# Turning the token tiles of two feed-forward stages without the matrix engine

## The reference

```python
x = x + 0.5 * ffn(layernorm(x), weight, bias, lora_A, lora_B, starts)
x = x + attention(layernorm(x), wq_a, q_a_ln_w, wq_b, wkv_a, kv_a_ln_w, wkv_b, wo)
x = x + 0.5 * ffn(layernorm(x), weight, bias, lora_A, lora_B, starts)

def ffn(x, ...):            # x is (2, 1024, 1024)
    y = x @ weight.T + bias
    lo = (x @ A.T) @ Bw.T   # rank 16, the adapter is chosen per batch
    return y + lo if the batch uses an adapter else y
```

## Time and profile before

| | |
|---|---|
| median of 3 runs | 1862.01 us (1861.92 to 1864.57) |
| the profiled execution: its time, its span | 1863.24 us, 1861.4 us |
| PE busy | 1783.3 us, 96% of the span |
| DVE, ACT, POOL busy | 66%, 54%, 44% |
| mean granted clock of PE | 0.987 |
| first stage, tile 2's matmuls to tile 15's | 69.75 to 241.97 us |
| second stage, the same | 1692.87 to 1857.62 us |
| DMA | 216.29 MB, 35.7% of 16 engines' span |

### The profile page before, as it was taken

One profiled execution on the slowest core, in us unless ns is written; L12 is line 12 of the kernel. 1 busy time (PEld: TensorE's weight loads), 2 busy tenths in 40 slices (PEclk: granted clock), 3 DMA queues, 4 the chain that ended last, 5 costly groups with the idle time before them and its releaser, 6 DMA issues. The chain is left out here.

```text
span 1861.4 us, 43728 instructions
## 1 busy us (share of the span) xinstructions
PE 1783.3 (96%) x15472; PEld 1416.4 (76%) x15472; DVE 1221.7 (66%) x2454; ACT 1007.1 (54%) x2137; POOL 813.6 (44%) x585
## 2 busy tenths in 40 slices
PE   5999969999999999999999999998899999989999
PEld 4788869877777777777777777775688888867887
DVE  5655448688887888878888787888533344435552
ACT  2221037788888888888888888887200001112110
POOL 3231211376766767667676676764200000024211
PEclk9999979999999999999999999999999999999999
DMA  6542162322222222212222122226855555525321
GB/s 215 199 163 102 60 178 92 75 82 59 65 87 66 74 57 64 87 61 79 57 64 87 56 83 57 64 81 210 306 181 196 202 206 207 193 91 168 126 90 57
DMA packets 141152, 216.29 MB, mean 116 GB/s; under 512 B 28192, under 2 KB 97952, under 8 KB 139040
## 3 DMA queue, kind: packets, MB, share of 16 engines
q1 hardware_dynamic: 141088, 215.43, 35.7%
HBM read 139.10 MB, written 76.28 MB: 116 GB/s over the span
## 5 line engine op out<-in xcount | busy, mean ns | idle before, releaser
L1318 PE MATMUL psS<-keyT,q 128*128 128x512 f32 (+2 forms) x2304 | 462.5, 349 | 12.4 <-issue 3.5
L1318 PEld LDWEIGHTS psS<-keyT,q 128*128 128x128 f32 x2304 | 377.6, 190 | 95.0 <-issue 33.1
L1436 DVE CUSTOM_DVE_ANT_0 prob<-psS,mask 128x640 f32<-128x640 f32 (+7 forms) x512 | 380.2, 750 | 80.2 <-PE psS L1318 55.3
L1385 ACT ACTIVATE prob<-prob,negmax 128x640 f32<-128x640 f32 (+7 forms) x512 | 393.2, 769 | 66.8 <-DVE negmax L1436 62.5
L1446 DVE STREAM_TRANSPOSE pT<-prob 128x640 f32<-128x640 f32 (+7 forms) x512 | 375.1, 761 | 81.9 <-PE psV L1335 77.4
L1111 PE MATMUL psS<-o_w,o_o 128*128 128x512 f32 x1536 | 350.8, 390 | 7.5 <-DVE o_w L1079 4.6
L1111 PEld LDWEIGHTS psS<-o_w,o_o 128*128 128x128 f32 x1536 | 288.8, 188 | 69.2 <-issue 7.4
L469 PE MATMUL f_psy<-f_weff,f_xT 128*128 128x512 f32 x1344 | 315.6, 393 | 0.0
L469 PEld LDWEIGHTS f_psy<-f_weff,f_xT 128*128 128x128 f32 x1344 | 250.8, 188 | 55.8
L1335 PE MATMUL psV<-pT,val 32*64 32x512 f32 (+3 forms) x8192 | 264.9, 407 | 4.7 <-DVE pT L1446 4.7
L633 POOL TENSOR_TENSOR pT<-pT,cosT 64x512 f32<-64x512 f32 x124 | 160.1, 1291 | 244.8 <-ACT pT L628 235.4
(11 more groups left out here) (118 smaller groups left out, 1710.7 us busy)
## 6 DMA issues: line engine op xcount, KB each, us to landing
o_parts<-pT SPq DMA_DIRECT2D x128, 256.0 KB, 3.0
wo<-in_wo SPq DMA_DIRECT2D x16, 1024.0 KB, 5.0
o_in<-o_parts SPq DMA_DIRECT2D x32, 512.0 KB, 6.7
o_o<-o_parts SPq DMA_DIRECT2D x32, 512.0 KB, 7.3
o_o<-row_scales SPq DMA_DIRECT2D x32, 512.0 KB, 8.2
f_xt<-in_x SPq DMA_DIRECT2D x16, 512.0 KB, 4.3
f_w_in<-in_w SPq DMA_DIRECT2D x16, 512.0 KB, 6.2
w_sum<-f_w_in SPq DMA_DIRECT2D x16, 512.0 KB, 5.3
```

Of the source, the lines that this page charges most:

```text
L1318: ins = nc.tensor.matmul(psS[:, slot, start + x0:start + x1], q[:, e, a, t * P:(t + 1) * P], k.keyT[:, m, b * S + x0:b * S + x1], start=(i ...
L1385: nc.scalar.activation(row, row, ACT.Exp, bias=negmax[:, n % 8:n % 8 + 1], scale=-1.0, accum_out=rowsum[:, column(n, s):column(n, s) + 1]) ...
L1436: nc.vector.tensor_tensor_reduce(out=prob[:, n % RING, 0:width], in0=place(n), in1=k.mask[:, S - width:S], scale=-1.0, scalar=LARGEST, op0 ...
```

## The change

Tiles 0 and 1 are still turned on PE. For tiles 2 to 15 of each stage the turning is made from three others:

- x is loaded with its rows in another order (`load_x` with `c a d`): partition 4c + a holds token 32a + c.
- DVE normalises into `normal[j]`. Four SBUF-to-SBUF transfers of 128 KB each (`move`) copy 256 columns of all 128 partitions into one strip of 32 partitions. DVE then turns each 32x32 block (`flip`). After it partition 32q + r holds feature 256q + 32t + r of the tokens.
- ACT takes the high part from `normal[j]` in SBUF, POOL the low part. DVE had it before.

The weights are laid out on the host in the same order of features, and tiles 0 and 1 are normalised into it. `xo` is no longer made from `f.xt`: x is loaded a second time into `xo[j]` (`load_sum`), and POOL adds the bias in place. So `f.xt` is free earlier, and x is loaded four tiles ahead. In the first stage there is one buffer `normal` and one for the strips; in the second there are two buffers `normal` and a new tensor for the strips. Some semaphores of set-up code are merged. The core of the diff:

```diff
@@ class Front / ffn_phase @@
-        nc.vector.tensor_scalar(self.xn[:, j, :], self.xt[:, j, :], self.mv[:, j, 0:1], self.rstd[:, j, :],
+        nc.vector.tensor_scalar(self.xn[:, j, :].rearrange("p (t q r) -> p q t r", q=GROUPS, t=DT),
+                                self.xt[:, j, :].rearrange("p (q t r) -> p q t r", q=GROUPS, t=DT), self.mv[:, j, 0:1], self.rstd[:, j, :],
                                 ALU.subtract, ALU.mult).then_inc(self.normed, 1)
...
+        if early is None:
+            normal, strips, ahead = (f.xn[:, 0, :], f.xn[:, 0, :]), f.xn[:, 1, :], 1
+        else:
+            normal, strips, ahead = (f.xn[:, 0, :], f.xn[:, 1, :]), c.sb(tag + "strips", [P, D])[:], 2
...
+        def turned_over(j, g):
+            return normal[j].rearrange("p (a t c) -> p t a c", a=GROUPS, t=DT)[:, 4 * g:4 * g + 4]
+        def split(j, part, g):
+            return f.xT[:, j, part, 4 * g:4 * g + 4, :].rearrange("p t (a c) -> p t a c", a=GROUPS)
@@ sync @@
             def load_x(m, jm):
-                sp.dma_start(f.xt[:, jm, :], src_d[bass.ds(m * P, P), :]).then_inc(f.x_in[jm], 16)
+                rows = src_d[bass.ds(m * P, P), :]
+                if later(m, 2):
+                    rows = rows.rearrange("(a c) d -> c a d", a=GROUPS)
+                sp.dma_start(f.xt[:, jm, :], rows).then_inc(f.x_in[jm], 16)
+            def load_sum(m, jm):
+                sp.dma_start(xo[:, jm, :], src_d[bass.ds(m * P, P), :]).then_inc(xo_in[jm], 16)
+            def move(m, jm):
+                sp.wait_ge(f.normed, m + 1)
+                if later(m, 3):
+                    sp.wait_ge(flipped, m - 2)
+                for q in range(GROUPS):
+                    sp.dma_start(strips[32 * q:32 * q + 32, :],
+                                 normal[jm][:, WIDTH * q:WIDTH * q + WIDTH]).then_inc(moved, 16)
...
+                if i == 6:
+                    move(2, 0)
+                    load_x(4, 0)
             def step(n, j, b, pieces, has):
...
-                if has(3):
-                    sp.wait_ge(f.normed, n + 2)
-                    sp.wait_ge(with_bias, n + 2)
-                    load_x(n + 3, (j + 1) % 2)
+                if has(2):
+                    move(n + 2, j)
+                if has(4):
+                    load_x(n + 4, j)
+                if has(1):
+                    sp.wait_ge(stored[(j + 1) % 2], loads_of(n - 1, (j + 1) % 2 if later(n, 2) else 0))
+                    load_sum(n + 1, (j + 1) % 2)
                 for i in pieces:
                     renew(i)
@@ gpsimd @@
             def add_bias(n, j):
+                if later(n, 2):
+                    pool.wait_ge(xo_in[j], (n - j) * 8)
+                    nc.gpsimd.tensor_tensor(xo[:, j, :], xo[:, j, :], bias_half[:], ALU.add).then_inc(with_bias, 1)
+                    return
...
             def step(n, j, b, pieces, has):
+                jm = (j + 1) % 2
+                if has(1):
+                    for g in range(2):
+                        pool.wait_ge(f.hi, n * 2 + g + 3)
+                        nc.gpsimd.tensor_tensor(split(jm, LO, g), turned_over(jm, g), split(jm, HI, g).bitcast(F32),
+                                                ALU.subtract).then_inc(f.lo, 1)
                 pieces_low(pieces)
                 if has(1):
-                    add_bias(n + 1, (j + 1) % 2)
+                    add_bias(n + 1, jm)
@@ scalar @@
                 if has(1):
-                    f.split_hi(nc, act, n + 1, (j + 1) % 2, product, 2)
+                    jm = (j + 1) % 2
+                    act.wait_ge(product, n * 2)
+                    act.wait_ge(flipped, n)
+                    for g in range(2):
+                        nc.scalar.activation(split(jm, HI, g), turned_over(jm, g), ACT.Copy).then_inc(f.hi, 1)
@@ tensor @@
             def step(n, j, b, pieces, has):
-                if has(1):
-                    f.turn(nc, pe, k.ident, n + 1, (j + 1) % 2)
@@ vector @@
+            def normalised(n, j):
+                f.invert(nc, dve, n, j)
+                dve.wait_ge(f.lo, (n - ahead) * 2 + 2)
+                dve.wait_ge(f.inv, n + 1)
+                nc.vector.tensor_scalar(normal[j], f.xt[:, j, :], f.mv[:, j, 0:1], f.rstd[:, j, :],
+                                        ALU.subtract, ALU.mult).then_inc(f.normed, 1)
+            def flip(n, j):
+                dve.wait_ge(moved, (n - 1) * 16 * GROUPS)
+                nc.vector.transpose(normal[j], strips).then_inc(flipped, 1)
...
             def step(n, j, b, pieces, has):
                 if not later(n, 2):
                     results(0, 0)
-                if has(1):
-                    f.split_lo(nc, dve, n + 1, (j + 1) % 2)
+                if has(2):
+                    normalised(n + 2, j)
                 make_pieces(pieces)
-                if has(2) and later(n, 2):
-                    f.stats_of(nc, dve, n + 2, j, loads_of(n + 2, j))
-                    dve.wait_ge(f.turned, n * 2 + 2)
-                    f.normalise(nc, dve, n + 2, j)
-                results(n, j)
+                if has(3):
+                    f.stats_of(nc, dve, n + 3, jm, loads_of(n + 3, jm))
+                results(n, j, [0])
+                if has(2):
+                    flip(n + 2, j)
+                results(n, j, [1])
```

More of the change, by code:

```diff
@@ L98, in constants_phase @@
         c = Ctx(nc, stack)
-        cleared, made = c.sem("c_cleared"), c.sem("c_made")
+        made = c.sem("c_made")
         block = stack.enter_context(nc.Block())
@@ L187, in split_lo @@
                                     ALU.subtract).then_inc(self.lo, 1)
+GROUPS = P // 32
+WIDTH = D // GROUPS
 def loads_of(n, j):
@@ L251, in ffn_phase @@
         bias_in, halved = c.sem(tag + "bias_in"), c.sem(tag + "halved")
-        w_stored = [c.sem(tag + f"w_stored{j}") for j in range(SLOTS)]
-        outer, summed, w_hi = c.sem(tag + "outer"), c.sem(tag + "summed"), c.sem(tag + "w_hi")
+        moved, flipped = c.sem(tag + "moved"), c.sem(tag + "flipped")
+        xo_in = [c.sem(tag + f"xo_in{j}") for j in range(2)]
+        if w_d is not None:
+            w_stored = [c.sem(tag + f"w_stored{j}") for j in range(SLOTS)]
+            outer, summed = c.sem(tag + "outer"), c.sem(tag + "summed")
+        w_hi = c.sem(tag + "w_hi")
         w_lo = [c.sem(tag + f"w_lo{j}") for j in range(2)]
@@ L345, in add_bias @@
             def add_bias(n, j):
+                if later(n, 2):
+                    pool.wait_ge(xo_in[j], (n - j) * 8)
+                    nc.gpsimd.tensor_tensor(xo[:, j, :], xo[:, j, :], bias_half[:], ALU.add).then_inc(with_bias, 1)
+                    return
                 pool.wait_ge(f.x_in[j], loads_of(n, j))
-                if later(n, 2):
-                    pool.wait_ge(stored[j], (n - j) * 8)
-                elif w_d is not None:
+                if w_d is not None:
                     pool.wait_ge(gate, B)
@@ L509, in gate_of, with results @@
                 nc.vector.tensor_scalar(gated[:, b, :], lora_a, chosen[:, b:b + 1], None, ALU.mult).then_inc(gate, 1)
-            def results(n, j):
+            def normalised(n, j):
[7 more added lines that the diff above has]
+                nc.vector.transpose(normal[j], strips).then_inc(flipped, 1)
+            def results(n, j, halves=range(2)):
                 dve.wait_ge(with_bias, n + 1)
-                for half in range(2):
+                for half in halves:
                     dve.wait_ge(product, n * 2 + half + 1)
@@ L542, in _ @@
                     f.stats_of(nc, dve, i - 1, (i - 1) % 2, loads_of(i - 1, (i - 1) % 2))
-                if i in (5, 6):
-                    dve.wait_ge(f.turned, 2 * (i - 4))
-                    f.normalise(nc, dve, i - 3, (i - 3) % 2)
+                if i == 5:
+                    normalised(2, 0)
+            flip(2, 0)
             def step(n, j, b, pieces, has):
@@ L736, in _ @@
                                     pattern=[[-1, P]], channel_multiplier=1).then_inc(mask_made, 1)
-            pool.wait_ge(mask_made, 1)
+            pool.wait_ge(mask_made, 2)
             pool.wait_ge(k.tab_in, 48)
```

18 lines of the change are left out of this document (9 added, 9 removed).

## The result

| | before | after |
|---|---|---|
| median | 1862.81 us of 4 runs (1861.92 to 1864.57) | 1876.20 us of 4 runs (1873.59 to 1876.99) |
| profiled execution: time, span | 1863.24, 1861.4 us | 1876.99, 1875.2 us |

What follows compares the result with a forecast made beforehand. PE was taken to bound the kernel; the second stage would gain 12.4 us and the first, paced by a ring without PE, lose 2.1. That is 10.3 less than 1863.24, 1852.9; the predicted median is 1851.7, range 1841.0 to 1863.5.

Steps and rivals of the forecast that it cites:

- the ring: First stage: a closed circle of waits without PE, from low parts through strips and `load_sum` to bias; 12.8 us a pass.
- PE for L424: Sign for the first stage: PE idles once a tile until POOL's low parts; tiles about 13 us apart, 12.8 in the loop.
- `load_sum` in the loop: First stage: the second load of x takes 4.6 us from issue to landing, with bounds of 3.4 and 6.9.
- the strips land later than 2.5 us: Sign for the first stage: strips landing later than 2.5 us after their issue would mean a longer ring.
- four issues took 1.67 us, so 0.42 each: Price of SP's transfer issues, taken from an earlier trace; four strip issues were put at 1.7 us of the ring.
- the entry of the ring: First stage, entered at step 2: the low parts of tile 3 were to start at about 74.5 us.
- 12.4 us were promised: Second stage: gain from 12 turns of 0.87 us leaving PE, an earlier x and tile 2 starting earlier.
- The tile-2 start: Second stage: tile 2 starts 0.3 us earlier, as turns leave but low parts follow a flip and two POOL instructions.
- (c): First stage: `load_sum` takes 6.9 us instead of 4.6, or low parts 1.9 instead of 1.29 each; total 1879; chance 0.1.
- (a): First stage: the ring is shorter than 11.9 us and PE sets the pace; gain 21.6, total 1840.4; chance 0.2.
- (b): First stage: strips drain slowly, `load_sum` lands 0.9 us later twelve times; total 1862.5, no change; chance 0.12.
- (d): Second stage: part of the gain stays away because flips or low parts are late; at half, 1858; chance 0.08.

Runs made afterwards that it cites:

- e4: The change with each strip copied straight, 128 partitions x 256 columns to the same columns (turn left out, tiles wrong): 1869.8 us, ratio 1.0032.
- e8: The change with each first-stage strip sent as two transfers of half the partitions, eight issues a tile instead of four: 1908.3 us, ratio 1.0254.
- e11: The change with one 128 x 1024 transfer for the four first-stage strips (turn across partitions left out, tiles wrong): 1852.7 us, ratio 0.9943.
- e2: The change with POOL adding the bias of tile n after the low parts of n+1, instead of the bias of n+1: 1860.2 us, ratio 0.9983.
- e9: e5 with second-stage tile 2 normalised ahead of tile 3's statistics, its strips issued after weight piece 4 instead of 6: 1844.6 us, ratio 0.9902.
- e1: The change with SyncE issuing `load_sum` ahead of the four strips and the x load, in both stages: 1858.2 us, ratio 0.997.
- e5: The change with `load_sum` ahead of the strips in the first stage only, and the bias after the low parts in the second: 1850.4 us, ratio 0.9933.
- e7: The change with the four first-stage strips issued from ScalarE's queue instead of SyncE's: 1891.0 us, ratio 1.0148.
- e10: e9 with one of two weight pieces summed before tile 3 is normalised, in step 1 of the first stage: 1844.3 us, ratio 0.9892.

## Why the prediction was wrong

**The mechanism held.** The second stage runs without turns or idle time, the first runs in the ring that was written out, the bias row is idle for `f_xo`, PE for L424. The terms low parts (2.53 measured, 2.55 said), normalising (0.81, 0.8), `load_sum` in the loop (173.97 to 178.55, 4.6 said) and bias (2.40, 2.45) were right, and so was the price of the flip (1245 ns, 1.24). Two of its signs read wrongly, though. In the steps with pieces PE's wait is for DVE's sum and not for L424, and "the strips land later than 2.5 us" came true (3.2) without making the ring longer, since e4 brought them to 2.1 and the pass hardly moved.

**The step that failed is "four issues took 1.67 us, so 0.42 each".** The earlier trace rows are four small transfers out of the attention; a strip's issue took 0.60 in the median (552 to 612 ns over 52 of them), four of them 2.49. Both are issued back to back from SyncE, so what differs is the transfer: those of the earlier trace rows carry 1.0 KB each, a strip carries 128 KB (no run has a size between 1 and 64 KB). A row much closer to the strips stood in the trace of before, 32 loads of 64 KB onto 32 partitions each, at 17.53 / 32 = 0.55 us apiece, or 2.2 for four:

```profile
row_scales<-rinvT SPq DMA_DIRECT2D x4, 1.0 KB
```

```profile
359.13 17.53 SPq L1218 DMA_DIRECT2D val<-values  x32
```

Four transfers in a row from SP in the first stage are less clear:

```profile
71.23 0.33 SPq L281 DMA_DIRECT2D f_xt<-in_x  x1
71.61 0.42 SPq L291 DMA_DIRECT2D w_sum<-f_w_in  x1
72.13 0.38 SPq L285 DMA_DIRECT2D f_w_in<-in_w  x1
72.56 1.29 SPq L291 DMA_DIRECT2D w_sum<-f_w_in  x1
```

From the first to the end of the fourth these are 73.85 - 71.23 = 2.62 us, but three of them agree with 0.42 and only the fourth is long, so that this nears the price of the strips may be chance. In a ring of twelve passes this one price counts 12 x 0.8 = 9.6 us. The load of x behind them took 0.96 us to the next issue in the loop instead of 0.6. That makes the measured pass 14.0 where the prediction had 12.8:

| term | said | measured |
|---|---|---|
| low parts, to the normalising's start | 2.6 | 169.47 - 166.90 = 2.57 |
| normalising, to the first strip | 0.85 | 0.84 |
| four strip issues | 1.7 | 173.01 - 170.31 = 2.70 |
| x, to the issue of `load_sum` | 0.6 | 0.96 |
| `load_sum` | 4.6 | 4.58 |
| bias | 2.45 | 2.35 |

e8 and e11 show this as cause and not as a coincidence: three issues fewer bring the start of the second stage forward by 25.1 us (1653.60 against 1678.70), four more put it off by 30.6.

**The whole first stage.** Tile 15 started at 251.06 instead of 232.7: 18.4 us. Of these 1.3 came from the entry of the ring (75.8 instead of 74.5), and 17.0 from the passes (172.7 against 155.7). Issues and register gaps, at about 1.0 a pass, are 12 of the 17. The other 5 are mostly in four longer passes: 15.8, 15.5 and 16.4 us among the weight pieces, and 14.65 in the loop. Two things make them up. In the passes of 15.8 and 14.65 SyncE's issue of the load of x, behind the strips, took 1.85 and 1.79 us instead of 0.60 to 0.65: 2.4 us together. And over the twelve passes the landings of `load_sum` add up to 62.6 us where 59.7 was allowed, mainly because it landed 6.6 us after its issue in the pass of 15.5 and 7.5 in the longest, from 150.49 to 166.90. There the store of a piece's sum was right behind it in the queue, but so it was in the pass before, where it landed in 5.5. These five are read from the trace alone, and their cause stays open; no run takes the stores away.

**The second stage.** 12.4 us were promised, 7.2 came. The tile-2 start, which I had 0.3 us earlier, came 2.4 us later relative to the stage's start. I had let the flip and two POOL instructions replace the turns, and had seen what POOL does to a normalising, but applied it only to the steady part, where it is hidden. At the start it isn't: 3.04 us instead of 0.8, the four strips behind it (3.06 us to issue there), then the flip. e2, where the normalising took 0.81 us and PE's idle time was 2.99 us, and e9, which starts it earlier, bear that out. The other 2.4 are pace: the steady part took 155.05 us, not 152.7. The windows view, first of the change from its start of tile 2, then of e9 around its own at 1685.87 (us, then busy us and instructions of PE, PEld, DVE, ACT and POOL, granted clock, DMA share, GB/s):

```profile
1716.00:1718.00 2.00, 1.75 (x4) 1.46 (x5) 2.00 (x3) 0.00 (x0) 2.00 (x2) 0.50 0.63 179
1718.00:1720.00 2.00, 2.00 (x6) 1.52 (x6) 1.26 (x3) 0.29 (x1) 1.51 (x1) 0.50 1.11 149
```

```profile
1685.00:1715.00 30.00, 29.13 (x128) 24.13 (x129) 22.82 (x29) 7.44 (x14) 21.67 (x12) 1.00 0.89 281
```

After 5.42 us of idle time the granted clock was 0.50, the lower level of 1.2 GHz, from 1716 to 1720, and 1.00 again from 1722; after 2.39 us in e9 it was 1.00, the full 2.4 GHz. With 2.4 us of slower matmuls behind 5.42 us of idle time, this idle time is paid about one and a half times. In the first stage 211.19 is such a tile, with 13.02 us instead of 11.44 and a clock of 0.50 from 213 to 215, but the one at 197.53, after a longer idle stretch (2.45 against 2.23 us), isn't: what tells them apart stays open.

**The rivals.** (c), slower by a longer ring, is what happened, and its deciding point (1.2 us a pass) was passed by 0.2; but it named the landing of `load_sum` and strided low parts; the low parts were as forecast, and the landings exceeded theirs by 2.9 us of the 17. No rival had the issue cost, though it was the one term of the ring priced from transfers of another kind. (a) and (b) are excluded by the idle rows and by e4. (d) came half true.

## What to carry to other kernels

When a change adds a load or a buffer dependence, write the circle of waits out and price every member; in a circle each tenth of a microsecond is paid once per tile, the issues of small transfers most of all, so take an issue's price from transfers of like size and shape, issued back to back in the same queue, and ask whether the landing at its end can be asked for before them. Here moving one issue ahead of four (e1) turned 13 us lost into a first stage bound by TensorE again, and with the second stage's start drawn forward (e9) the same idea that was 0.7% slower is 1.0% faster than before. But an order that opens one stage's ring can put a wait in another where there was none.

## What the hardware showed unexpectedly

- Strips of 128 KB issued back to back from one queue take 0.60 to 0.63 us each to issue: the same for 32 destination partitions, for 16 with half the bytes, and for a straight copy over all 128 (e4). One transfer of 512 KB in their place took 0.50 us in the median (e11), four of 1.0 KB in the attention 1.67 us together (before). The load of the sum took 0.33 us where nothing had been issued just before it (e1, e5) and 0.59 right behind the load of x (the change, outside the loop).
- A transfer within SBUF that writes 32 partitions lands in 3.2 us, one of the same bytes that writes all 128 in 2.1 (e4). The Trainium skill (SBUF — State Buffer, section on the DMA port swizzle) has 32 partitions reach half of the ports. The sign agrees; what was slower was the landing, and the landing wasn't in the ring.
- Small transfers moved to a second queue landed later, not earlier: 6.8 us against 3.2 (e7), while big loads of the first queue went beside them.
- A normalising of DVE took 3.0 us when POOL's low part of 128x1024 began 0.07 to 0.09 us after it by the profile (nine runs), and 0.81 us when it began 0.13, 0.15 or 0.21 us after it (e10, before, e2).
